# Perceiver block on one NeuronCore: the column maximum moved from TensorE to GpSimd, the rounding of splits from GpSimd to ScalarE

## The reference

```
x = x + cross_attention(layernorm(x), context)   # 16 heads of 64, keys and values from 1601 context rows
x = x + linear_attention(layernorm(x))           # 8 heads of 64; softmax over d of q, over n of k
x = x + moe_ffn(layernorm(x))                    # router, 8 experts of 256 -> 1024 -> 256, top 2 of 8 weighted
```

## Time and profile before

| | us |
|---|---|
| median of 3 runs | 975.37 |
| the profiled execution, whole | 972.43 |
| its span, first to last instruction | 970.6 |
| TensorE matmul busy | 925.1 |
| VectorE busy | 735.5 |
| ScalarE busy | 502.7 |
| GpSimd busy | 561.5 |
| first and last copy of the maximum to mbc | 69.87 and 676.75 |

### The profile page before, as it was taken

The page is one execution under the profiler, slowest core; times in us unless marked ns, Lnnn a source line. Parts: engine busy times, 40 slices in busy tenths (PEclk is TensorE's granted clock), DMA queues, the critical chain, the costliest instruction groups (busy, mean ns, idle before and its releaser), DMA issues.

```text
span 970.6 us, 18294 instructions
## 1 busy us (share of the span) xinstructions
PE 925.1 (95%) x6116; PEld 794.2 (82%) x6116; DVE 735.5 (76%) x1147; ACT 502.7 (52%) x856; POOL 561.5 (58%) x590
## 2 busy tenths in 40 slices
PE   6999999999999999999999999999998699999998
PEld 3568888888888888888888888888786487888887
DVE  4659778787977978788787787875776767887776
ACT  3556656565565555656555565654452333344332
POOL 5729778678948957876894795730000442444440
PEclk9999999999999999999999999999999899999999
DMA  5872122212211212221221121101004022222200
GB/s 162 282 246 56 53 59 59 58 44 59 63 40 55 70 37 61 58 62 39 57 70 34 52 67 47 49 9 66 1 2 174 5 96 74 88 87 86 86 1 22
DMA packets 75084, 66.41 MB, mean 68 GB/s; under 512 B 7920, under 2 KB 71680, under 8 KB 75008
## 3 DMA queue, kind: packets, MB, share of 16 engines
q1 hardware_dynamic: 75008, 65.37, 22.2%
HBM read 57.48 MB, written 7.86 MB: 67 GB/s over the span
## 4 chain that ended last, share of the span: by engine, by line
PE 84%; DVE 11%; ACT 3%; issue 2%; POOL 0%; DMA 0%; SPq 0%; DVEq 0%; ACTq 0%; POOLq 0%
PE sps L1194 28%; PE scp L1212 9%; PE scp L1214 9%; PE scp L1213 9%; PE scp L1409 5%; PE sps L1395 4%; PE wps L1395 4%; PE scp L1410 3%; DVE u_sb L910 2%; PE wps L1239 2%; DVE st L875 1%; PE sps L1307 1%; PE scp L1162 1%; PE sps L1148 1%; DVE cmax L886 1%
## 5 line engine op out<-in xcount | busy, mean ns | idle before, releaser
L1212 PE MATMUL scp<-cn,pt_hi 128*128 128x258 f32 (+1 forms) x832 | 239.3, 288 | 4.4 <-DVE pt_lo L900 3.7
L1213 PE MATMUL scp<-cn,pt_hi 128*128 128x256 f32 (+1 forms) x832 | 234.9, 282 | 0.0
L1214 PE MATMUL scp<-cn,pt_lo 128*128 128x258 f32 (+1 forms) x832 | 234.7, 282 | 0.0
L900 DVE TENSOR_TENSOR pt_lo<-st,pt_hi 128x512 fp32r<-128x512 f32 (+1 forms) x208 | 196.7, 945 | 6.8 <-ACT pt_hi L670 6.8
L661 ACT ACTIVATE st<-sps 128x512 f32<-128x512 f32 (+1 forms) x208 | 123.4, 593 | 149.7 <-PE sps L1194 148.8
L875 DVE TENSOR_TENSOR st<-st,mbc 128x512 f32<-128x512 f32 (+1 forms) x208 | 158.7, 763 | 38.5 <-ACT mbc L684 38.0
L1194 PE MATMUL sps<-qk_hi,ct_hi 128*128 128x512 f32 (+1 forms) x416 | 168.3, 405 | 13.7 <-DVE cmax L886 5.7
L667 ACT ACTIVATE st<-st 128x512 f32<-128x512 f32 (+1 forms) x208 | 130.3, 626 | 88.1 <-DVE st L875 87.4
L1212 PEld LDWEIGHTS scp<-cn,pt_hi 128*128 128x128 f32 (+1 forms) x832 | 156.9, 189 | 14.5 <-DVE pt_lo L900 6.6
L1194 PE MATMUL sps<-qk_hi,ct_lo 128*128 128x512 f32 (+1 forms) x416 | 164.2, 395 | 0.0
L1194 PE MATMUL sps<-qk_lo,ct_hi 128*128 128x512 f32 (+1 forms) x416 | 163.4, 393 | 0.0
(11 more groups left out here) (209 smaller groups left out, 1433.6 us busy)
## 6 DMA issues: line engine op xcount, KB each, us to landing
w_raw<-W SPq DMA_DIRECT2D x16, 1024.0 KB, 7.4
raw<-ctx_t SPq DMA_DIRECT2D x96, 128.0 KB, 2.2
raw<-ctx_n SPq DMA_DIRECT2D x96, 128.0 KB, 2.0
raw<-qk_scratch SPq DMA_DIRECT2D x56, 128.0 KB, 2.0
qk_scratch<-stage_b SPq DMA_DIRECT2D x4, 896.0 KB, 4.8
qk_scratch<-stage_a SPq DMA_DIRECT2D x4, 896.0 KB, 4.7
wq_sb<-w_q SPq DMA_DIRECT2D x1, 1024.0 KB, 5.0
wkt_sb<-w_kt SPq DMA_DIRECT2D x1, 1024.0 KB, 7.8
```

Of the source, the lines that this page charges most:

```text
L900: dve.tensor_tensor(pt_lo[0:rows(j), r, :], st[0:rows(j), par, j, :], pt_hi[0:rows(j), r, :].bitcast(F32), ALU.subtract).then_inc(lo_ok, 1)
L1212: pe.matmul(scp[:, t, 0:D + 2], hi, cn[0:rows(j), j, 0:D + 2], start=j == 0, stop=False)
L1213: pe.matmul(scp[:, t, 0:D], hi, cn[0:rows(j), j, D + 2:CNW], start=False, stop=False)
L1214: ins = pe.matmul(scp[:, t, 0:D + 2], lo, cn[0:rows(j), j, 0:D + 2], start=False, stop=j == SJ - 1)
```

## The change

- `transpose_max`, `spread_max`, `column_max` and `take_max` are gone. GpSimd does `all_max` ahead of the jobs of a group's first slot: it waits for the finished `cmax`, runs a one-column add (`mtouch`) and then one `partition_all_reduce` of 128 x 512, whose result goes to `mbc`.
- The hi part of a job that belongs to a slot is made on ScalarE (`high_part`, at the end of ScalarE's slot); GpSimd makes only its lo. The first 26 jobs, ahead of slot 0, stay on GpSimd.
- RR goes from 4 to 6; UNIT_LEAD, the number of slots between a context job and the scores of its unit, from 6 to 5; L_SUB, L_LO and L_PV grow by one, and so do the once-a-group steps.
- All `Fori` loops are written out.

```diff
-L_SUB, L_LO, L_PV = SJ + 4, SJ + 5, SJ + 6
+L_SUB, L_LO, L_PV = SJ + 5, SJ + 6, SJ + 7
-V_MT, V_MR, V_MB, V_MC = 1, 2, 3, 3
-V_U, V_UT, V_UTC, V_WV, V_O = 5, 6, 7, 8, 9
-RR = 4
+V_U, V_UT, V_UTC, V_WV, V_O = 6, 7, 8, 9, 10
+RR = 6
-UNIT_LEAD = 6
+UNIT_LEAD = 5
...
+                else:
+                    pool.wait_ge(slot_hi, hi_count + 1 - len(FIRST_JOBS))
                 pool.tensor_tensor(lo, src, hi.bitcast(F32), ALU.subtract).then_inc(done, 1)
...
+            def all_max(g, par):
+                pool.wait_ge(max_ok, (g + 1) * SJ)
+                pool.tensor_tensor(mtouch[:], cmax[:, par, 0:1], zero[:], ALU.add)
+                pool.partition_all_reduce(mbc[:, par, :], cmax[:, par, :], P, bass.bass_isa.ReduceOp.max)\
+                    .then_inc(mbc_ok, 1)
 
             def split_pass(i, of):
                 for u in range(PASS):
+                    if u % SJ == 0 and not (of == 0 and u == 0):
+                        all_max(linear(i, lambda q: q * (PASS // SJ) + u // SJ - 1), (u // SJ - 1) % 2)
                     for job in slot_jobs(of * PASS + u):
-                        split_job(shift(job, -of), i)
+                        split_job(shift(job, -of), i, False)
...
+            def high_part(job, i):
+                src, hi, _ = split_views(job, i)
+                may_split(act, job, i)
+                act.activation(hi, src, ACT.Copy).then_inc(slot_hi, 1)
...
             for u in range(PASS):
                 slot(0, u, u)
+                split_slot(0, 0, u)
...
-            with act.Fori(0, NPASS - 1) as i:
+            for i in range(1, NPASS):
                 for u in range(PASS):
                     slot(i, u, PASS + u)
+                    split_slot(i, i, u)
```

More of the change, by code:

```diff
@@ L212, in build @@
         lnT_lo = sb("lnT_lo", [P, DT, TOK], F32R)
-        mcol = sb("mcol", [P, GT])
+        mtouch = sb("mtouch", [P, 1])
         rsum = sb("rsum", [P, GT])
@@ L517, in load_pass @@
                         load_job(shift(job, -of), i)
[L519 to L522, removed]
+            for i in range(NPASS):
+                load_pass(i, i)
             sp.wait_ge(scores_ok, NSLOT)
@@ L537, in _ @@
             load_expert(1, 0, 1)
-            with sp.Fori(1, NE // 2) as i:
+            for i in range(1, NE // 2):
                 load_expert(i * 2, i, 0)
@@ L565, in _, with split @@
                       allow_small_or_imprecise_dtypes=True).then_inc(eidx_ok, 1)
[L566 to L572, removed]
+            def split(src, hi, lo, hi_count, done, both):
+                if both:
+                    z = zero[0:src.shape[0], :]
+                    for _ in range(len(src.shape) - 2):
+                        z = z.unsqueeze(1)
+                    pool.tensor_tensor(hi, src, z.broadcast_to(tuple(src.shape)), ALU.add).then_inc(split_hi, 1)
+                    pool.wait_ge(split_hi, hi_count + 1)
+                else:
+                    pool.wait_ge(slot_hi, hi_count + 1 - len(FIRST_JOBS))
@@ L589, in _ @@
-            with pool.Fori(0, NPASS - 2) as i:
-                split_pass(i, 1)
-            split_pass(NPASS - 1, NPASS - 1)
+                split_job(job, 0, True)
+            for i in range(NPASS):
+                split_pass(i, i)
+            all_max(NG - 1, (NG - 1) % 2)
             def chain_rstd(m, which):
@@ L611, in _ @@
                 low_weights(0, 1, part)
-            with pool.Fori(1, NE // 2) as i:
+            for i in range(1, NE // 2):
                 for s in range(2):
@@ L799, in _ @@
             experts(0, 1, (1, 0))
-            with act.Fori(1, NE // 2 - 1) as i:
+            for i in range(1, NE // 2 - 1):
                 experts(i, 0, (i, 1))
@@ L926, in slot @@
                     running_max(i, u - 1)
-                if u % SJ == V_MR and SJ <= k < NSLOT + SJ:
-                    column_max(i, u)
                 if u % SJ == V_U and k >= 2 * SJ:
@@ L943, in _ @@
                     first_low(LATE_TILE[u - 1])
-            with dve.Fori(0, NPASS - 1) as i:
+            for i in range(1, NPASS):
                 for u in range(PASS):
@@ L1121, in _ @@
             expert(0, 1)
-            with dve.Fori(1, NE // 2 - 1) as i:
+            for i in range(1, NE // 2 - 1):
                 expert(i, 0)
@@ L1222, in transpose_u @@
                     else:
[L1223 removed]
+                        wait(pe, utc_ok, linear(i, lambda q: (q * (PASS // SJ) + u // SJ - 2) * 2))
                     for a in range(2):
@@ L1281, in _ @@
                     make_qk(LATE_TILE[u])
-            with pe.Fori(0, NPASS - 1) as i:
+            for i in range(1, NPASS):
                 for u in range(PASS):
@@ L1467, in _ @@
                 y_tile(1, 2, f, 1)
-            with pe.Fori(1, NE // 2 - 1) as i:
+            for i in range(1, NE // 2 - 1):
                 expert(i, 0)
```

51 lines of the change are left out of this document (9 added, 42 removed).

## The result

The changed kernel takes 1024.82 us (median of 4 runs, 1023.98 to 1025.94) against 975.08 for the kernel before in the same session: 1.051 times as long, 95% interval 1.0491 to 1.0524. The profiled execution took 1025.66 us, its span is 1023.8.

The account below looks back on a forecast made before the run. TensorE was taken to bound the kernel (matmuls fill 95% of the span). 972.4 - 14.4 (transposes) - 3.0 (lag) + 7 (roundings) = 962, + 74 (GpSimd's absence) = 1036, as a median 1039 us; 8-in-10 range 963 to 1115.

Parts of the forecast that it names:

- What GpSimd's absence does: Once a group, in 13 groups: ScalarE stops at the seventh deferred job's raw load, stalling TensorE at slot 6; +74 us.
- the cover of 12.2 us: From a group's start, GpSimd's absence is hidden up to 17.0 - 4.8 = 12.2 us; any excess stalls TensorE in full.
- W: How long GpSimd is away per maximum: `mtouch` 0.2, program load 7, reduction 3.7, load back 7; 17.9 us.
- binds later: Where next jobs are `ct`, slot 5's scores also wait for the first lo (T0 + W + 0.93 against 14.2).
- The Trainium skill's rule: First call to a freshly loaded GpSimd kernel pays about 6 us of instruction load; W 15.9, sum 1010 us.
- Transposes: Transposes for the maximum leave TensorE, four each way: 0.9 us a group, 16 times, -14.4 us.
- GpSimd's lag at a group's start: TensorE's late group starts, put down to GpSimd's splits, end when it loses the hi parts: -3.0 us.
- Loops: Writing out the loops: branches cost nothing findable in the waits, so zero.
- ScalarE's roundings behind U: New roundings ahead of the copy of scores, after U is taken from PSUM: 0.5 us at 14 places, +7 us.
- The drain: The end of the kernel: put at zero, 3 us either way, with raw buffers, leads and loops.
- the serial rival: The reduction on GpSimd goes column by column, 51 us: near 1740 us, or 1930 by the skill's 62 us; chance 0.04.
- The other rivals: Cheap program loads, W about 4.5 us, 965 us, chance 0.18; ScalarE's roundings delaying every slot, 1029 us, 0.09; serial reduction, 0.04.

Follow-up runs that it names:

- with the clock held up: The changed kernel plus eight unused matmuls on TensorE where each group stalls (slot 5 in even groups, 6 in others): 1017.4 us, ratio 1.0437.
- the fastest kernel: The kernel with lo parts on VectorE, plus weight transfers three slots later, an early one-column reduction and a final one-column addition: 956.44 us, ratio 0.9816.

## Why the prediction was right, and where it was not

It said 1039 us, slower, range 963 to 1115; it is 1024.8. The mechanism is right, and the nearness of the number is in part luck. By its own steps:

- **What GpSimd's absence does: right.** The stop of ScalarE at the seventh job, the stall at slot 6, the 13 groups, and the cover of 12.2 us are what the traces show. With the mean W of 15.6 us the formula (W less the cover) gives a stall of 3.4 us, and 3.4 was measured with the clock held up. Eight raw buffers take the path away. Only "binds later" for the `ct` jobs needs a word: in seven of the 13 groups TensorE stands first at slot 5, for 2.1 us, and the rest follows at slot 6, 0.6 to 0.7 us where the clock is held up.
- **W: 17.9 said, 15.6 measured in the mean.** This is the mis-sized term. The reduction was put at 3.7 us and takes 1.9; the load ahead of it was put at 7 and takes 5.9; the load behind it was put at 7 and takes 7.2; `mtouch` was put at 0.2 and takes 0.57. Term: 74 us said, 13 x 3.4 = 44 measured.
- **The Trainium skill's rule ("GPSIMD Engine Reference", Instruction dispatch).** The trace has 5.90 and 6.76 us of idle time around the reduction shown. The Trainium skill's about 6 us is that size: by it the prediction put W at 15.9, closer to the 15.6 measured than its own 17.9. The Trainium skill does not say there when a load is due; here one comes at each change of kind, twice a group, and those ahead of the first and the last reduction are longer (10.71 and 8.29 us).
- **Transposes: right.** 0.9 us a group said; 40.29 - 39.39 = 0.90 between the kernel that makes the maximum with transposes and the one that makes none over partitions.
- **GpSimd's lag at a group's start: the 3.0 us are there, the cause is another.** The 0.93 us that I read stand at a turn of the loops, and they and the 1.98 us at the next turn go when the loops are written out: 3.2 us. With the splits still on GpSimd and the loops written out, no group starts late.
- **Loops: zero said, 4 us gained.** 3.2 of them are what I had put down to GpSimd.
- **ScalarE's roundings behind U: wrong.** +7 us said. The wait there is 0.22 us in the changed kernel against 0.81: it got shorter, by 0.6 us in every second group, 3 to 4 us in all. The hi splits of the earlier blocks no longer run on GpSimd, and `pt_lo` on VectorE takes 719 ns against 945 before; which of these moved the slot I did not separate.
- **The start: missed.** I wrote that the start of group 1 has few jobs. It has the first `qk` load, behind ten weight transfers, and an in-order engine with other work was put in front of it; GpSimd's first load of the reduction's programs (10.71 us) ends at the same place. Both had to go for the start to be as short as before (60.4 us for the first two groups, against 60.2).
- **The drain: missed.** "Behind group 15 there are no jobs" was true and not enough: `rstd` is behind it on GpSimd. 10 us.
- **The clock: missed.** About 10 us in the middle groups, as a consequence of the stall.
- **A figure of the serial rival.** A reduction of 62 us gives near 1905 us by the prediction's own sum, not 1930. Nothing rests on it.

The sum without the reduction was 962.0 for a profiled execution; that with the addition in its place took 960.5. That is luck: the 7 us for the roundings are not there, and the start, for which the sum had nothing, costs 6.6 (103.79 against 97.17). The 65 us on top are 44 of stall, 10 to 11 of clock and 12 of drain, less 1 at the start. I had 74 for the first alone: a stall too long by 30 us stood in for two terms that I did not have (clock and drain, 22 us), and so the total is closer than its parts. That is luck as well. The other rivals fell plainly: loads are not cheap, the reduction is not serial, and ScalarE has room.

## What to carry to other kernels

Ask of a moved instruction not how long it takes but how long its engine is away for it, and what is queued behind it there: here 1.9 us of work kept the engine away for 15.6, and the stall was that less the cover of the buffers, 12.2. An engine whose instructions are of two kinds that change programs should get all of one kind, if another engine has room for the rest (VectorE was busy 65% of the span and 76% with them); that turned 1.051 into 0.987. When two things end at one place, taking away one shows nothing: take away both before you call either harmless.

## What I had not expected of the hardware

- A change between elementwise instructions and the reduction over partitions costs GpSimd 5.8 to 6.1 us one way and 6.8 to 7.8 back, each time, in the 13 middle groups; the time is on record as idle, "issue". The first in the program took 10.7 us when issued at 65 us (10.0 to 11.1 in the other kernels that issue it at 64 to 65), and 5.8 us when issued at 57 us; why is open. Memset does not bring it on: between the memset at 298.55 and the reduction at 298.62 there is no idle time.
- The reduction of 128 x 512 is recorded with 1.8 to 2.1 us where it follows such a change, and 1.8 to 2.3 behind another reduction. With the lo parts on VectorE and no change ahead it took 3.06 us in the middle groups, but 1.8 in the last group and in the first of the fastest kernel. Why is open.
- A stall of 2 to 3 us can bring TensorE to 1.2 GHz in the slot behind it: mean 0.62 in the window of 4.47 us, and after the stall of 2.57 us at 338.60 the clock stayed at 1.00. In the changed kernel it fell after ten of the 13 stalls, and the longer ones at slot 6 brought it down less often (three of six) than those at slot 5 (seven of seven); what decides I cannot tell. Eight matmuls in the stall left no such slot in 12 of the 13 groups.
- One of VectorE's instructions is shorter in the kernels in which GpSimd is busy less: the lo of the weights took 945 ns with GpSimd busy 58% of the span (944 with the loops written out), 719 with 35%, and 683 with 18% (lo parts on VectorE). The running maximum, which reads PSUM, did not change (680 and 686 ns). Where GpSimd alone was given more to do (the reduction twice) the lo took 766. The reason is not shown. The kernel before, the changed one and the one with lo parts on VectorE:

```profile
L900 DVE TENSOR_TENSOR pt_lo<-st,pt_hi 128x512 fp32r<-128x512 f32 (+1 forms) x208 | 196.7, 945 | 6.8 <-ACT pt_hi L670 6.8
```

```profile
L903 DVE TENSOR_TENSOR pt_lo<-st,pt_hi 128x512 fp32r<-128x512 f32 (+1 forms) x208 | 149.5, 719 | 1.5 <-ACT pt_hi L675 1.5
```

```profile
L912 DVE TENSOR_TENSOR pt_lo<-st,pt_hi 128x512 fp32r<-128x512 f32 (+1 forms) x208 | 142.0, 683 | 1.1 <-ACT pt_hi L673 1.1
```
